# Macaron block on one core: weighed feed-forward rows added to the token rows by scatters, and slots of 512, 512, 512, 256, 256 and 128 rows

## What is computed

```python
x = x + 0.5 * ffn(layernorm(x), w_router, w_fc, w_proj)
x = x + attention(layernorm(x), Wq, Wk, Wv, Wg, Ws, Wo, g_norm_weight)
x = x + 0.5 * ffn(layernorm(x), w_router, w_fc, w_proj)
```

## Time and profile before

| | before |
|---|---|
| median of 3 runs | 2157.71 us (2156.02 to 2160.22) |
| the profiled execution | 2169.04 us |
| its span, first to last instruction | 2167.5 us |
| its mean granted TensorE clock | 0.979 |
| first feed-forward, about | 0 to 454 us |
| attention, about | 454 to 1721 us |
| last feed-forward, about | 1721 to 2167 us |

### The profile page before, as it was taken

The page is one execution under the profiler, slowest core; times in us unless marked ns, Lnnn a source line. Parts: engine busy times, 40 slices in busy tenths (PEclk is TensorE's granted clock), DMA queues, the critical chain, the costliest instruction groups (busy, mean ns, idle before and its releaser), DMA issues. The chain is left out here.

```text
span 2167.5 us, 30602 instructions
## 1 busy us (share of the span) xinstructions
PE 2022.1 (93%) x11728; PEld 1662.0 (77%) x11728; DVE 1399.8 (65%) x2607; ACT 669.2 (31%) x1156; POOL 281.6 (13%) x242
## 2 busy tenths in 40 slices
PE   2999999959999999999999999999998598999996
PEld 2788888857887878878878878878887387888885
DVE  5675666767666665666666666666677565666657
ACT  3444444534121222212221221212222143444443
POOL 3100001031020020110110110201202103000003
PEclk9999999989999999999999999999999699999998
DMA  5342333530010010000100100100001234342337
GB/s 213 136 146 95 129 107 131 165 117 8 1 37 9 8 31 8 18 28 1 37 9 1 37 9 1 37 8 15 23 1 39 95 111 112 122 136 97 120 127 229
DMA packets 46911, 149.22 MB, mean 69 GB/s; under 512 B 5824, under 2 KB 5824, under 8 KB 46784
## 3 DMA queue, kind: packets, MB, share of 16 engines
q1 hardware_dynamic: 38544, 121.13, 17.3%
q0 software_dynamic: 8240, 26.24, 3.6%
HBM read 125.31 MB, written 22.04 MB: 68 GB/s over the span
## 5 line engine op out<-in xcount | busy, mean ns | idle before, releaser
L1245 PE MATMUL at_pj<-at_w_lo,at_xT_hi 128*128 128x512 f32 x512 | 210.2, 410 | 0.0
L1245 PE MATMUL at_pj<-at_w_hi,at_xT_hi 128*128 128x512 f32 x512 | 200.8, 392 | 0.0
L1245 PE MATMUL at_pj<-at_w_hi,at_xT_lo 128*128 128x512 f32 x512 | 200.7, 392 | 0.0
L1219 PE MATMUL at_pj<-at_xT_hi,at_w_lo 128*128 128x512 f32 x384 | 158.9, 414 | 13.0 <-issue 12.2
L580 DVE TENSOR_TENSOR last_ff_w_lo<-last_ff_stage,last_ff_w_hi 128x1024 fp32r<-128x1024 f32 x80 | 98.0, 1225 | 96.5 <-ACT last_ff_w_hi L413 96.5
L580 DVE TENSOR_TENSOR first_ff_w_lo<-first_ff_stage,first_ff_w_hi 128x1024 fp32r<-128x1024 f32 x80 | 98.0, 1225 | 90.6 <-ACT first_ff_w_hi L413 90.5
L1219 PE MATMUL at_pj<-at_xT_hi,at_w_hi 128*128 128x512 f32 x384 | 152.2, 396 | 0.0
L1219 PE MATMUL at_pj<-at_xT_lo,at_w_hi 128*128 128x512 f32 x384 | 152.1, 396 | 0.0
L862 POOL TENSOR_TENSOR at_coef<-at_ms,minus_half 128x4 f32<-128x4 f32 x64 | 63.5, 1009 | 558.1 <-DVE at_ms L1177 558.1
L677 PE MATMUL last_ff_ps_h<-last_ff_xT_hi,last_ff_w_lo 128*128 128x512 f32 (+1 forms) x320 | 120.2, 376 | 13.7 <-issue 12.0
L838 POOL TENSOR_TENSOR at_w_lo<-at_stage,at_w_hi 128x1024 fp32r<-128x1024 f32 (+1 forms) x36 | 78.5, 2181 | 397.7 <-ACT at_w_hi L902 397.7
(11 more groups left out here) (307 smaller groups left out, 4770.2 us busy)
## 6 DMA issues: line engine op xcount, KB each, us to landing
first_ff_stage<-wff SPq DMA_DIRECT2D x80, 512.0 KB, 3.5
last_ff_stage<-wff SPq DMA_DIRECT2D x80, 512.0 KB
at_stage<-watt SPq DMA_DIRECT2D x24, 512.0 KB, 3.6
at_stage<-watt SPq DMA_DIRECT2D x16, 384.0 KB, 3.2
xres<-x SPq DMA_DIRECT2D x4, 1024.0 KB, 10.0
first_ff_xg<-sorted_rows SPq DMA_DIRECT2D x4, 1024.0 KB, 6.3
slot_rows<-first_ff_y POOLq DMA_DIRECT2D x4, 1024.0 KB, 6.7
last_ff_xg<-sorted_rows SPq DMA_DIRECT2D x4, 1024.0 KB, 6.2
```

What stands on the lines that cost most here:

```text
L1219: last = pe.matmul(PJ[(7 * k + part) % 2][:, :], wq(w, kk, part), x[:, kk, tok], start=(kk == 0 and n == 0), stop=(kk == KC - 1 and n == 2))
L1245: last = pe.matmul(PJ[(7 * k + 3 + t) % 2][:, :], x[:, kk, tok], wvg(w, kk), start=(kk == 0 and n == 0), stop=(kk == KC - 1 and n == 2))
```

## The change

- The slots have 512, 512, 512, 256, 256 and 128 rows (2176 in all), all written out, no `Fori`. The last one, `EDGE`, is computed in plain float32 without splitting: per hidden tile `up_edge` has 4 products of 128 columns and `down_edge` one of 512 columns, both straight from the loaded weight tile. Its weight tiles have a ring of seven: the four of `stage` and three in the room of `xn_rest`. A tile is loaded again when `down_edge` has used it.
- Rows get two more columns (`W = D + 2`): the router gap and the token number. They travel with the row through `sorted_rows` into `xg`. `weigh` computes from them the row's weight (zero where the row belongs to the other expert) and its destination, six small DVE operations and one ACT `Exp` per slot, at t = 1, 2 and 4. The evictions multiply by that weight.
- POOL adds each 128 rows of `y` to `dest` by an indirect DMA with an add. `dest` is `mid_rows` (DRAM) in the first and `out` in the last feed-forward. SP stores the 4 MB of `xres` to `dest` beforehand, in four DMAs of 1 MB between the last four weight loads of slot 0; POOL waits for them before its first add.
- The attention loads `xres` back from `mid_rows` on SP: four DMAs of 256 KB, then three of 1 MB. Its gathers and adds go, and so do `weights`, the marks, `finish`, `add_row`, and the stores of `slot_rows` and `out`.
- In slot 0, SP's waits and the load of the next slot's rows move from load t = 8 to t = 12. There and in the other slots SP also waits for `weight_done`.

```diff
-SLOTS = GROUPS + 1
-BLOCK = GROUP // 2
+WIDTHS = (GROUP, GROUP, GROUP, GROUP // 2, GROUP // 2, P)
+SLOTS = len(WIDTHS)
+EDGE = SLOTS - 1
+W = D + 2
+EDGE_RING = 7
...
+            def edge_loads(tile0):
+                for t in range(RING, HT):
+                    if t >= EDGE_RING:
+                        sp.wait_ge(down_done, EDGE * HT + RING + t - EDGE_RING + 1)
+                    load_w(tile0, t, edge_stage[t % EDGE_RING], t % EDGE_RING)
...
-                    if after and t == 2 * RING:
+                    if t == (3 if first_slot else 2) * RING:
                         sp.wait_ge(x_turned, j * KC + KC)
+                        sp.wait_ge(weight_done, j + 1)
...
+                    if first_slot and t >= HT:
+                        g = t - HT
+                        sp.dma_start(dest.rearrange("(i p) d -> p i d", p=P)[:, tiles(g), :], xres[:, tiles(g), :]).then_inc(base_stored, 16)
...
-                pool.dma_start(slot_rows[bass.ds(to, width), :].rearrange("(i p) d -> p i d", p=P), y[:, 0:width // P, :]).then_inc(y_stored, 16)
-                pool.wait_ge(y_stored, j * 16 + 16)
+                if j == 0:
+                    pool.wait_ge(base_stored, 16 * (TILES // RT))
+                pool.wait_ge(weight_done, j + 1)
...
+                for i in range(width // P):
+                    pool.indirect_dma_start(out=dest, out_offset=bass.IndirectOffsetOnAxis(ap=to_row[:, j % 2, i:i + 1], axis=0),
+                                            in_=y[:, i, 0:D], in_offset=None, compute_op=ALU.add).then_inc(y_added, 16)
+                pool.wait_ge(y_added, 16 * tiles_before[j + 1])
                 pool.sem_inc(y_free, 1)
...
+            def weigh(j, width, t):
...
+                if t == 1:
+                    dve.wait_ge(x_loaded, 16 * j + 16)
+                    dve.scalar_tensor_tensor(out=mag[:, b, 0:count], in0=xg[:, 0:count, D], scalar=-1.0, in1=xg[:, 0:count, D], op0=ALU.mult, op1=ALU.max).then_inc(mag_done, 1)
+                    dve.tensor_scalar(mine[:, b, 0:count], xg[:, 0:count, D], 0.0, expert, ALU.is_lt, ALU.is_equal)
+                    dve.tensor_copy(to_row[:, b, 0:count], xg[:, 0:count, D + 1])
+                if t == 4:
+                    dve.wait_ge(em_done, j + 1)
+                    step(dve.tensor_scalar(em[:, b, 0:count], em[:, b, 0:count], 1.0, None, ALU.add))
+                    step(dve.reciprocal(weight[:, b, 0:count], em[:, b, 0:count]))
+                    dve.scalar_tensor_tensor(out=weight[:, b, 0:count], in0=weight[:, b, 0:count], scalar=0.5, in1=mine[:, b, 0:count],
+                                             op0=ALU.mult, op1=ALU.mult).then_inc(weight_done, 1)
...
+                def up_edge(t):
...
+                    for k in range(KC):
+                        if t == 0:
+                            pe.wait_ge(x_hi_done, j * KC + k + 1)
+                        last = pe.matmul(ps_h[t % 2][:, 0:P], edge_stage[n][:, k * P:(k + 1) * P], xe[:, k, :], start=(k == 0), stop=(k == KC - 1))
...
+                def down_edge(t):
...
+                    pe.matmul(ps_y[0][:, :], edge_a(t), edge_stage[t % EDGE_RING][:, D:2 * D], start=(t == 0), stop=(t == HT - 1)).then_inc(down_done, 1)
...
         def _(sp):
+            from_mid = mid_rows.rearrange("(i p) d -> p i d", p=P)
+            for t in range(UC):
+                sp.dma_start(xres[:, t, :], from_mid[:, t, :]).then_inc(row_loaded[t], 16)
+            for m in range(1, UNITS):
+                sp.dma_start(xres[:, tiles(m), :], from_mid[:, tiles(m), :]).then_inc(rows_loaded[m - 1], 16)
```

More of the change, by code:

```diff
@@ L109, in place @@
     dve.tensor_tensor(r["row_i"][:, at], r["base"][:, at], r["behind"][:, at], ALU.add).then_inc(rows_ready, 1)
-    step(dve.tensor_tensor(r["pos"][:, at], r["base"][:, at], r["behind"][:, at], ALU.add))
 def early_slot(dve, step, r, slot_table, n, ready):
@@ L228, in phase_feed_forward, with held, normed, edge_a @@
         with_slot = [g for g in steps if g >= 2]
-        KNOWN = GROUPS + 1
+        KNOWN = 3
+        tiles_before = [sum(w // P for w in WIDTHS[:j]) for j in range(SLOTS + 1)]
+        act_copied = [sum((w // P + 1) // 2 for w in WIDTHS[:j]) for j in range(SLOTS + 1)]
+        dve_copied = [sum(w // P // 2 for w in WIDTHS[:j]) for j in range(SLOTS + 1)]
         tiles = lambda g: slice(g * RT, (g + 1) * RT)
         piece_step = HT // (len(PIECES) - 1)
-        takes_piece = lambda j, t: x_in is not None and isinstance(j, int) and j == GROUPS - 1 and t % piece_step == 0
-        def normed(i):
-            if i < 2 * GT:
-                return (xg, y)[i // GT][:, i % GT, :]
-            return late_x[:, i - 2 * GT, :] if i < 2 * GT + 2 else xn_rest[:, i - 2 * GT - 2, :]
-        def all_slots(engine, slot_body):
-            slot_body(0, GROUP, GROUP)
-            with engine.Fori(1, GROUPS - 1) as j:
-                slot_body(j, GROUP, GROUP)
-            slot_body(GROUPS - 1, GROUP, BLOCK)
-            slot_body(GROUPS, BLOCK, 0)
+        takes_piece = lambda j, t: x_in is not None and j == EDGE - 3 and t % piece_step == 0
+        def held(g):
+            return ((xg, 0), (y, 0), (xn_rest, 0), (xn_rest, RT))[g]
+        def normed(i, width=D):
+            room, first = held(i // RT)
+            return room[:, first + i % RT, 0:width]
+        def edge_a(t):
+            return a[:, t % 2, (t // 2 % 2) * P:(t // 2 % 2 + 1) * P]
+        def all_slots(slot_body):
+            for j in range(SLOTS):
+                slot_body(j, WIDTHS[j], WIDTHS[j + 1] if j < EDGE else 0)
         @block.sync
@@ L482, in gaps @@
                     dve.wait_ge(xn_done, i - steps[0] * RT + 1)
-                    out = (square, square, factor, factor)[i % RT][:, i % 2, :] if g < 2 else (rows if x_in is not None else junk)[:, i % 2, :]
+                    out = (square, square, factor, factor)[i % RT][:, i % 2, :] if g < 2 else rows[:, i % 2, :] if x_in is not None else xn_rest[:, i % 2, 0:D]
                     last = dve.tensor_tensor_reduce(out=out, in0=normed(i), in1=wdiff[:], scale=1.0, scalar=0.0,
@@ L486, in gaps, with mark @@
                 return last
+            def mark(g):
+                room, at = held(g)
+                dve.tensor_copy(room[:, at:at + RT, D], gap[:, tiles(g)])
+                dve.tensor_copy(room[:, at:at + RT, D + 1], tok[:, tiles(g)])
             def route(g, before=None):
@@ L593, in _ @@
             split_x(0, GROUP, 0, KC)
-            behind_by = 3
-            def add_row(i):
-                dve.wait_ge(loaded[i % GATHERS], loaded_before[i % GATHERS] + 16 * (i // GATHERS + 1))
-                dve.scalar_tensor_tensor(out=xres[:, i, :], in0=ring[i % GATHERS], scalar=half_weight[:, i:i + 1],
-                                         in1=xres[:, i, :], op0=ALU.mult, op1=ALU.add).then_inc(added, 1)
             def slot_body(j, width, after):
-                finishes = y_out is not None and not after
-                if finishes:
-                    dve.wait_ge(late_loaded, 16)
-                    dve.tensor_copy(late_i[:, :], late[:, :, 0]).then_inc(late_known, 1)
                 for t in range(HT):
-                    if t == 0:
+                    if t == 0 and j < EDGE:
                         split_w(j, AHEAD)
@@ L657, in turn_x @@
                 for k in range(k0, k1):
-                    if not first or k >= 2:
+                    if j == EDGE:
+                        pe.wait_ge(x_hi_done, j * KC + k - 1)
+                    elif not first or k >= 2:
                         pe.wait_ge(x_lo_done, j * KC + k - 1)
@@ L693, in down @@
                     last.then_inc(down_done, 1)
+                if j == EDGE:
+                    for t in range(HT + AHEAD):
+                        if t < HT:
+                            up_edge(t)
+                        if t >= AHEAD:
+                            down_edge(t - AHEAD)
+                    return
                 for t in range(AHEAD):
```

371 lines of the change are left out of this document (155 added, 216 removed).

## The result

The changed kernel takes 2143.59 us (median of six runs, 2137.09 to 2146.56) beside 2158.97 for the kernel before (six runs, 2156.02 to 2163.84): a ratio of 0.9923, 95% interval 0.9905 to 0.9942, some 15.4 us less. The forecast was 2119 with a range of 2098 to 2142: right in its sign, 25 us off in its size, and the result lies just outside the range. The profiled execution took 2142.46 us, span 2140.7.

A forecast was written before the change was run, and what follows sets the result against it. PE was taken to bound the kernel. First feed-forward -16.2, last -28.7 and +0.5 sum to -44.4 us: 2169.0 to 2124.6 for the profiled execution; for the median 2119, between 2113.3 and 2122.2, range 2098 to 2142.

The forecast's parts named there:

- my own rule for the latter: 512-column product of `down_edge`: the 128-column price scaled by columns, 0.03 of fixed cost kept apart, taken as 0.91 us.
- the rival of late weight tiles: Float32 block runs at its loads' pace, say 2.6 us a tile: +11 per block, about 2141; chance 0.07.
- DVE as the bound of the whole narrow slot: Rival: narrow slots don't hold 2.81 us a tile, DVE sets the pace: +11, about 2130; chance 0.10.
- The four passes: Trainium skill's count for a true float32 product; puts the `down_edge` product near 0.9 us, leaving the sum unmoved.
- Part 1: Feed-forward slots: one 512-row slot becomes a 256-row slot and a float32 block; first -9.1 us, last -17.9.
- Part 2: Adds, `xres` stores and SP's new wait for `weight_done` around the slots: all cost nothing.
- 0.5 us for copies: Attention, last pair of heads: twelve small DVE copies cost +0.5 us.
- Part 5: Handover to the attention: -2.0 us, plus -1.0 from relieving DVE of adds; -3.0 in all, bounds -5 to +3.
- Part 6: Tail: one eviction and one add instead of two, -1.9 us; also twelve small DVE copies, +0.5.
- Part 3: Slot 0 of the first feed-forward: moving SP's wait to t = 12 removes a PE stall and lower clock, -4.1 us.
- Part 4: End of slot 0 of the last feed-forward: stall and lower clock go with the mark scatters, -8.9; bounds -8.9 to 0.

The follow-up runs named there:

- experiments 1 and 4: Changed kernel with unused bytes padding both feed-forwards (1: 2131.5 us, ratio 0.9868), then its attention padded too, two small tensors moved (4: 2120.92 us, ratio 0.9814).
- experiment 6: Kernel before with only SyncE's waits and row load of slot 0 moved from tile 8 to tile 12: ratio 0.9989, 2.4 us less.

## Why the prediction was right and wrong

**Right.** The direction, by its reason: PE is the bound, and 128 slot rows less with half of the late slot in plain float32 shortens its work. The narrow slots had the right form: 48.5 and 47.1 us once the queue is free, 47.8 and 47.9 forecast. The block was dear by 2.7 us in my sum: 16 tiles at 1.75 us instead of 1.90 (four products of 128 columns in 0.89 us, one of 512 in 0.86; my own rule for the latter gives 0.90, not the 0.91 that I took). In the profile of the changed kernel the block runs at 1.75 us a tile to its end, so the rival of late weight tiles falls. DVE as the bound of the whole narrow slot falls with the 48.5 and 47.1 us; it is waited for at each slot's start. The four passes that the Trainium skill gives for float32 (FP8 and Floating Point Precision, TensorE Precision Notes) make 4 x 1024 columns a tile, by estimate 1.71 us if one column takes one cycle of 2.4 GHz, and the trace agrees with its 1.75.

**Wrong.** By its steps:

- *Part 1, "88.8, 88.1".* I carried the untouched slots over at their old duration. They grew by 2.4 to 2.5 us, six of them, 14.8 us, and with them half of the products of the narrow slots. The cause was in the diff, in the line that makes a row 514 words and so moves the transposed rows by 32 bytes against the weights. In the attention the two tensors that the change drops did the same. There I had 0.5 us for copies; the profiles differ by 4.9, of which some 3.4 is spacing and most of the rest the clock of those two executions. It is the largest miss: the padding of experiments 1 and 4 gave back 12.1 and 10.6 us (about 6 of the latter the kernel before had also been paying).
- *Part 2, "over when SP comes to it: nothing".* True in the slots of 512 rows, false in the first narrow one, where SP stood 6.6 us. Moving the wait gave 3.9 us in the four narrow slots of the profile, 6.0 between medians of two sets. I had compared tile numbers of the slot of 512 rows and not repeated it at half the pace.
- *Part 2, the adds, "nothing".* True between slots; 1.5 us at the handover and 2.1 in the tail. Part 5 had counted the longer landing as 2 us later, yet its net of -3.0 was -1.2: the variances came 17.3 us after PE's last product, forecast 16 (its own 18.1 less 16.3 makes -1.8, not the -2.0 in the sum). Part 6 erred the other way: -1.9 forecast, -4.3 measured, adds included.
- *Part 3, -4.1.* The wait behind the row load is real and moving the load removes it, but the term was read off one profile, with a wait of 2.43 us and 1.7 us of lower clock behind it. Six later profiles have 1.8 to 1.9 us and no lower clock, and the step alone gave 2.4 us between medians (experiment 6). In the changed kernel's profile only 0.8 us is left of it: 2.4 went to the spacing and about one to a low clock at slot 0's first products.
- *Part 4, -8.9.* The stall is real, its cause was the suspected coincidence of the mark scatters, and the change removes it: slot 0 of the last took 96.8 us, 2.1 over the 94.7 forecast, which is about the spacing of one slot. But by their times the runs of record had it in the profiled execution only. For that case the forecast itself said 2122.2 us. Against a kernel before at 2170 us the changed one would gain 26 to 28, not 15: that compares medians of different sets, since the changed kernel was not run in a set where the kernel before took 2170; its two medians agree within 2 us.

In the two profiled executions the sum missed 17.7 us (44.4 - 26.7): the spacing 14.8 in the six slots, the attention 4.4, the narrow slots 3.4 (2.0 and 2.4 in the first ones, of which the held queue is 1.4 and 1.6, less 0.5 in each second one), the low clock 0.9, the handover 1.8, less 5.3 for the cheaper block and 2.4 for the tail, together 17.6. From 2122.2 to the median of 2143.6 it is 21.4. Of the other 4 us some 2 are part 3's, whose lower clock too only the one profile had; the rest lies between single executions and medians.

## What to carry to other kernels

A change of one tensor's size moves all tensors behind it: after such a change compare the spacing of products that were not touched, and if it differs with the granted clock the same, look at the distance of the two operands' addresses before anything else. A wait that is free in a long stage has to be timed anew in a short one, with all that stands behind it in its queue. And a stall or a lower clock that only one profiled execution shows should be priced with its chance, or looked at in a second profile, before it enters the sum: here that held for parts 3 and 4 alike.

## What the runs showed of the hardware

- Products of 512 float32 columns start 226.7 ns apart when the held and the streamed tensor start a multiple of 256 bytes apart, and 229 to 234 ns apart at distances of 32, 64, 128, 192 and 224 bytes: 3% of TensorE's time, at the granted clock of 1.00, moved both ways by padding alone (-12.1 us, +15 us). In one group of attention products some stayed at 231 ns at distance 0. It is the distance and not where one operand starts, and it is there while VectorE and ScalarE are idle too (232.5 ns).
- Sixteen small scatters issued from GpSimd, 1.26 us apart, went with ScalarE standing 14 us in some sets and not at all in others (2170 against 2160 us for one program); moving them took 9 us away. In both cases the DMA engines beside them moved 21 or 22 GB/s at a share of 0.97 to 1.02, and in the profile that shows it weight tiles landed after 9.4 us instead of 3.5.
- An indirect add of 128 rows is issued in 1.55 us, a plain indirect write in 0.96; with plain writes the handover was 1.3 to 1.8 us shorter and the tail 2.1.
